# The first attention group's score pieces and row maxima, moved into the QKV projection, and its operands transposed tile by tile

## The reference, cut to what matters

```python
x = L0_attn_hidden_states                      # (2, 1024, 512) f32
x = x + 0.5 * ffn(layernorm(x), w1, mean_w1, w2, mean_w2, w3, mean_w3)
x = x + attn(layernorm(x), w_qkv, b_qkv, w_dense, b_dense)
x = x + 0.5 * ffn(layernorm(x), ...same weights...)

# attn: 32 query heads, 8 key/value heads, head size 16
qkv = einsum('bsh,oh->bso', h, w_qkv) + b_qkv
q, k, v = split(qkv);  q, k = rope(q), rope(k)
scores = einsum('bqhd,bkhd->bhqk', q, k) / 16  # causal mask
probs  = softmax(scores)
out    = einsum('bhqk,bkhd->bqhd', probs, v) @ w_dense.T + b_dense
```

## Time and profile before

| | us |
|---|---|
| median of 3 runs | 1462.23 (1461.75 to 1462.47) |
| the profiled execution, its own time | 1461.78 |
| its span in the trace | 1460.1 |
| PE busy | 1375.6 (94%) |
| DVE busy | 1068.4 (73%) |
| ACT busy | 608.2 (42%) |
| POOL busy | 183.7 (13%) |

### The profile page before, as it was taken

How to read it: one execution, slowest core, us unless ns; L and a number is a source line. 1 busy time by engine, 2 the same in 40 slices (tenths; PEclk the granted TensorE clock), 3 DMA queues, 4 the chain that set the end, 5 groups by cost and what they waited for, 6 DMA issues and landing times.

```text
span 1460.1 us, 25505 instructions
## 1 busy us (share of the span) xinstructions
PE 1375.6 (94%) x9984; PEld 707.6 (48%) x9984; DVE 1068.4 (73%) x1611; ACT 608.2 (42%) x802; POOL 183.7 (13%) x269
## 2 busy tenths in 40 slices
PE   1899999999999996799999999999999999999997
PEld 0344444444444442233333333333577777777774
DVE  7999566764665587899999999965576666665544
ACT  5762123222211352287878777765222122222111
POOL 1000000000000363032323222211011011011000
PEclk9999999999999997599999999999999999999999
DMA  9702941021021012211111111030534647467440
GB/s 386 251 0 101 254 140 58 26 61 44 33 47 36 8 34 42 57 24 30 26 38 24 29 27 38 2 131 1 181 130 156 221 167 217 170 215 204 162 159 29
DMA packets 151980, 144.40 MB, mean 99 GB/s; under 512 B 129856, under 2 KB 133440, under 8 KB 148032
## 3 DMA queue, kind: packets, MB, share of 16 engines
q1 hardware_dynamic: 151872, 142.91, 31.2%
HBM read 96.73 MB, written 21.76 MB: 81 GB/s over the span
## 4 chain that ended last, share of the span: by engine, by line
PE 81%; DVE 11%; ACT 2%; issue 2%; SPq 2%; DMA 1%; POOL 0%; DVEq 0%; ACTq 0%; POOLq 0%
PE ps L2215 17%; PE ps L1778 17%; PE ps L2232 10%; PE ps L1989 9%; PE ps L1903 7%; PE ps L1799 6%; PE ps L1970 5%; PE ps L1893 3%; PE ps L1825 2%; PE ps L2087 2%; DVE rowmax L1534 2%; PE ps L1999 1%; PE ps L1907 1%; DVE blocks L1426 1%; SPq L522 1%
## 5 line engine op out<-in xcount | busy, mean ns | idle before, releaser
L955 ACT ACTIVATE probs<-ps 128x1024 f32<-128x1024 f32 (+3 forms) x384 | 292.5, 811 | 84.0 <-PE ps L1970 82.0
L1778 PE MATMUL ps<-xt_hi,w_all 128*128 128x512 f16 x896 | 274.8, 381 | 9.6 <-DVE w_all L1179 9.3
L2215 PE MATMUL ps<-xs,wpair 128*128 128x256 f16 x2352 | 261.3, 273 | 0.9 <-DVE second_sum L1661 0.9
L2215 PEld LDWEIGHTS ps<-xs,wpair 128*128 128x128 f16 x2352 | 230.1, 98 | 33.5 <-DVE second_sum L1661 1.1
L1534 DVE TENSOR_REDUCE rowmax<-ps 128x2 f32<-128x1024 f32 (+3 forms) x208 | 237.4, 1141 | 11.9 <-PE ps L1911 6.4
L1903 PE MATMUL ps<-ka,qa 48*128 48x512 f16 (+3 forms) x768 | 162.6, 347 | 25.8 <-DVE rowmax L1534 13.1
L1778 PE MATMUL ps<-xt_lo,w_all 128*128 128x512 f16 x448 | 170.5, 381 | 0.0
L1989 PE MATMUL ps<-probs,vs 128*32 128x512 f32 (+3 forms) x1536 | 164.9, 501 | 2.4 <-ACT ctx_sb L974 2.4
L1778 PEld LDWEIGHTS ps<-xt_hi,w_all 128*128 (+1 forms) x896 | 88.0, 98 | 117.4 <-issue 11.4
L1538 DVE TENSOR_REDUCE rowmax<-ps 128x1 f32<-128x512 f32 x192 | 131.1, 683 | 8.1 <-PE ps L1903 8.1
L2232 PE MATMUL ps<-wpair,hs_hi 128*128 128x512 f16 x448 | 133.2, 379 | 0.5 <-DVE hs_lo L1688 0.5
(11 more groups left out here) (168 smaller groups left out, 1811.3 us busy)
## 6 DMA issues: line engine op xcount, KB each, us to landing
wpair<-spill SPq DMA_DIRECT2D x28, 2304.0 KB, 8.9
spill<-block_parts SPq DMA_DIRECT2D x14, 512.0 KB, 2.7
spill<-w_all SPq DMA_DIRECT2D x24, 224.0 KB, 4.1
x<-x_in SPq DMA_DIRECT2D x4, 1024.0 KB, 5.3
y_out<-x SPq DMA_DIRECT2D x4, 1024.0 KB, 11.2
wbase<-m1t SPq DMA_DIRECT2D x4, 896.0 KB, 12.6
w_raw<-w1t SPq DMA_DIRECT2D x4, 896.0 KB, 14.2
wbase<-m3t SPq DMA_DIRECT2D x4, 896.0 KB, 24.2
```

Of the source, the lines that this page charges most:

```text
L955: nc.scalar.activation(probs[u % PBUF][:, 2 * pair:2 * pair + 2, 0:q1 - q0], wide(("scores", g, (u, pair)))[:, :, 0:q1 - q0], ACT.Exp, sca ...
L1778: last = mm(ps[:, bank, :], w[a][:, k, bass.ts(t, P)], xt[b][:, k, :], start=(k == 0 and n == 0), stop=(k == HB - 1 and n == 2))
L2215: last = mm(product_bank(n, i)[:, m, :], weight_of(n, m, a, weight, k), xs[c % 2][:, b, 2 * rows_ + k, :], start=(k == 0 and q == 0), stop ...
```

## The change

QKV tiles 10 to 15 on PE now contain pieces 0 to 16 of group 0: one before the second half of the tile, one after half of that half's matmuls, one behind the tile. DVE reduces pieces 0 to 20 in its loop over the tiles, three in each of the iterations 10 to 16. SP issues group 0's transposes tile by tile as the parts come, between the four pairs of transposes of chunk 7. Pieces 17 to 24 are made, and 21 to 24 reduced, where they were before. The code of each operation is the same; there are as many of each as before.

```diff
+EARLY_TILE = 10
+EARLY_TAKEN = 3 * (TOKEN_TILES + 1 - EARLY_TILE)
+EARLY_MADE = EARLY_TAKEN - 4
...
         sp.wait_ge(up_full, 4 * IT)
-        place_normal(7)
...
-        sp.wait_ge(qklo_ready, 2 * SEQ_TILES)
-        sp.wait_ge(qkhi_ready, 2 * SEQ_TILES)
-        sp.wait_ge(kpad_ready, 4 + SEQ_TILES)
+        def place_first(tt):
+
+            sp.wait_ge(qklo_ready, 2 * tt + 2)
+            sp.wait_ge(qkhi_ready, 2 * tt + 2)
+            sp.wait_ge(kpad_ready, tt + 1 + min(tt // 2 + 1, 4))
+            place_operand_tile(0, tt)
+
+        place_normal_tile(7, 0)
+        sp.wait_ge(qkv_full, 4)
+        place_first(0)
+        place_first(1)
+        place_normal_tile(7, 1)
+        place_first(2)
+        place_first(3)
+        place_normal_tile(7, 2)
+        place_first(4)
+        place_normal_tile(7, 3)
+        for tt in range(5, SEQ_TILES):
+            place_first(tt)
         ln_placed_by(sp, 7)
-        place_operands(0)
         place_operands(1)
...
+        def early(i, at_):
+
+            if i >= EARLY_TILE:
+                reduce_piece(0, 3 * (i - EARLY_TILE) + at_)
+
+        for i in range(TOKEN_TILES + 1):
+            if 3 <= i < 7:
+                normal_parts(7, i - 3)
+            if 1 <= i:
+                add_turned(i - 1)
+            early(i, 0)
+            if i < TOKEN_TILES:
+                along(i)
+            early(i, 1)
+            if 1 <= i:
+                low_parts(i - 1)
+            early(i, 2)
+            if i == 2:
+                norm_stats(7)
...
             for s in range(2):
+                if s:
+                    early_piece(3 * (i - EARLY_TILE) - 1)
...
+                    if s and k == 1:
+                        early_piece(3 * (i - EARLY_TILE))
             last.then_inc(qkv_full, 1)
-
-        for i in range(TOKEN_TILES):
-            qkv(i)
+            early_piece(3 * (i - EARLY_TILE) + 1)
...
+        def early_piece(r):
+
+            if 0 <= r < EARLY_MADE:
+                score_piece(0, r)
+
+        def later_piece(k, r):
+
+            if k or r >= EARLY_MADE:
+                score_piece(k, r)
```

More of the change, by code:

```diff
@@ L488, in _, with place_normal_tile @@
             .then_inc(wd_loaded, 16)
+        def place_normal_tile(n, j):
+            sp.wait_ge(xhi_ready, TPC * n + j + 1)
+            sp.wait_ge(xlo_ready, TPC * n + j + 1)
+            for i in range(2):
+                sp.dma_start_transpose(xt_of(n)[i][:, :, j * P:(j + 1) * P], ln_parts(j)[i])\
+                    .then_inc(ln_placed[n % 2], 16)
         def place_normal(n):
             for j in range(TPC):
[L493 to L497, removed]
+                place_normal_tile(n, j)
         sp.wait_ge(up_full, IT)
@@ L515, in _, with place_operand_tile @@
         sp.wait_ge(up_full, 4 * IT)
-        place_normal(7)
+        def place_operand_tile(g, tt):
+            b, i = divmod(g, KV_HEADS)
+            sp.dma_start_transpose(qa[g % BUF][:, :, tt * P:(tt + 1) * P],
+                                   parts_q[:, SEQ_TILES * b + tt, Q_PER_KV * i:Q_PER_KV * (i + 1), :].rearrange("p h c -> p (h c)"))\
+                .then_inc(qk_placed[g % BUF], 16)
+            if g % 2 == 0:
+                sp.dma_start_transpose(ka[g // 2 % BUF][:, tt * P:(tt + 1) * P].unsqueeze(1),
+                                       parts_k[:, SEQ_TILES * b + tt, i:i + 2, :].rearrange("p h c -> p (h c)"))\
+                    .then_inc(qk_placed[g % BUF], 16)
         def place_operands(g):
-            b, i = divmod(g, KV_HEADS)
             for tt in range(SEQ_TILES):
[L522 to L528, removed]
-        sp.wait_ge(qklo_ready, 2 * SEQ_TILES)
-        sp.wait_ge(qkhi_ready, 2 * SEQ_TILES)
-        sp.wait_ge(kpad_ready, 4 + SEQ_TILES)
+                place_operand_tile(g, tt)
+        def place_first(tt):
[15 more added lines that the diff above has]
+            place_first(tt)
         ln_placed_by(sp, 7)
-        place_operands(0)
         place_operands(1)
@@ L1501, in low_parts @@
                                     in1=parts_k[:, i, :, 0:HEAD], op=ALU.subtract).then_inc(qklo_ready, 1)
[L1503 to L1513, removed]
         def reduce_piece(k, r):
@@ new lines, in _ @@
+        for i in range(TOKEN_TILES + 1):
[13 more added lines that the diff above has]
+        def later_piece(k, r):
+            if k or r >= EARLY_TAKEN:
+                reduce_piece(k, r)
@@ new lines, in _ @@
+        for k in range(GROUPS):
+            later_piece(k, 0)
+            later_piece(k, 1)
+            later_piece(k, 2)
+            later_piece(k, 3)
+            later_piece(k, 4)
+            later_piece(k, 5)
+            later_piece(k, 6)
+            later_piece(k, 7)
+            later_piece(k, 8)
+            later_piece(k, 9)
+            later_piece(k, 10)
+            later_piece(k, 11)
+            later_piece(k, 12)
+            normalise(k - 2, 0)
+            later_piece(k, 13)
+            later_piece(k, 14)
+            later_piece(k, 15)
+            later_piece(k, 16)
+            later_piece(k, 17)
+            later_piece(k, 18)
+            later_piece(k, 19)
+            later_piece(k, 20)
+            later_piece(k, 21)
+            later_piece(k, 22)
+            later_piece(k, 23)
@@ L1604, in _ @@
             normalise(k - 2, 1)
-            reduce_piece(k, 24)
+            later_piece(k, 24)
             split_rowmax(k)
@@ L1945, in score_piece, with later_piece @@
             last.then_inc(single_full, 1)
+        def early_piece(r):
+            if 0 <= r < EARLY_MADE:
+                score_piece(0, r)
+        def later_piece(k, r):
+            if k or r >= EARLY_MADE:
+                score_piece(k, r)
+        for i in range(TOKEN_TILES):
+            qkv(i)
         def transpose_rowmax(g):
@@ L2003, in _ @@
             scores_t(k - 2, 6, 1)
-            score_piece(k, 0)
-            score_piece(k, 1)
+            later_piece(k, 0)
+            later_piece(k, 1)
             scores_t(k - 2, 7, 0)
             values(k - 2, 5)
-            score_piece(k, 2)
+            later_piece(k, 2)
             transpose_rowmax(k - 1)
             scores_t(k - 2, 7, 1)
-            score_piece(k, 3)
+            later_piece(k, 3)
             scores_t(k - 2, 8, 0)
             values(k - 2, 6)
-            score_piece(k, 4)
+            later_piece(k, 4)
             scores_t(k - 2, 8, 1)
             scores_t(k - 2, 9, 0)
-            score_piece(k, 5)
+            later_piece(k, 5)
             values(k - 2, 7)
             scores_t(k - 2, 9, 1)
-            score_piece(k, 6)
+            later_piece(k, 6)
             values(k - 2, 8)
-            score_piece(k, 7)
+            later_piece(k, 7)
             scores_t(k - 2, 10, 0)
-            score_piece(k, 8)
+            later_piece(k, 8)
             scores_t(k - 2, 10, 1)
@@ L2027, in _ @@
             scores_t(k - 2, 11, 0)
-            score_piece(k, 9)
-            score_piece(k, 10)
+            later_piece(k, 9)
+            later_piece(k, 10)
             scores_t(k - 2, 11, 1)
-            score_piece(k, 11)
+            later_piece(k, 11)
             values(k - 2, 10)
-            score_piece(k, 12)
+            later_piece(k, 12)
             scores_t(k - 1, 0, 0)
@@ L2036, in _ @@
             scores_t(k - 1, 0, 1)
-            score_piece(k, 13)
+            later_piece(k, 13)
             scores_t(k - 1, 1, 0)
-            score_piece(k, 14)
+            later_piece(k, 14)
             values(k - 2, 11)
-            score_piece(k, 15)
+            later_piece(k, 15)
             scores_t(k - 1, 1, 1)
             scores_t(k - 1, 2, 0)
-            score_piece(k, 16)
+            later_piece(k, 16)
             values(k - 1, 0)
-            score_piece(k, 17)
+            later_piece(k, 17)
             scores_t(k - 1, 2, 1)
             scores_t(k - 1, 3, 0)
-            score_piece(k, 18)
+            later_piece(k, 18)
             values(k - 1, 1)
             scores_t(k - 1, 3, 1)
-            score_piece(k, 19)
+            later_piece(k, 19)
             scores_t(k - 1, 4, 0)
-            score_piece(k, 20)
+            later_piece(k, 20)
             values(k - 1, 2)
-            score_piece(k, 21)
+            later_piece(k, 21)
             scores_t(k - 1, 4, 1)
-            score_piece(k, 22)
+            later_piece(k, 22)
             scores_t(k - 1, 5, 0)
             values(k - 1, 3)
-            score_piece(k, 23)
+            later_piece(k, 23)
             scores_t(k - 1, 5, 1)
@@ L2064, in _ @@
             scores_t(k - 1, 6, 0)
-            score_piece(k, 24)
+            later_piece(k, 24)
             values(k - 1, 4)
```

24 lines of the change are left out of this document (removed).

## The result

| | us |
|---|---|
| changed kernel, median of 6 runs | 1455.72 (1455.49 to 1456.23) |
| kernel before, median of 6 runs beside it | 1461.99 |
| ratio, 95% interval | 0.9949 (0.9936 to 0.9962) |
| profiled execution, its span | 1455.49, 1453.8 |

The account below looks back on a forecast made before the run. PE was taken to bound the kernel, except at the ends and in a hole at 560 to 620 us; group 1's first reduction coming 7.7 us earlier gave 1462.23 - 7.7 = 1454.5 us, range 1449 to 1458.5.

Parts of the forecast that it names:

- The place and the kind of the gain: Hole between QKV tiles and group pipeline: whole program moves with group 1's first reduction, 7.7 us earlier than 594.23.
- SP and the wait: Piece 0 in tile 10: SP's 24 transposes at 1.28 us land at 539.8, so PE waits 4.3 us.
- The clock inside tile 10: At PE's wait before piece 0: clock falls for 4 to 5 us, so PE does 2.1 us less.
- The woven tiles: Tiles 10 to 15: PE's and DVE's lists equally long, 1.2 us added for mutual waits, tile 15 ends at 573.2.
- The tail: Group 0 behind tile 15: 13.3 us to group 1's first reduction at 586.5, including 0.8 of waits.
- Group 1 unchanged: Group 1: clock expected to fall in group 0's tail, so group 1 takes 28.4 us as before, gain 0.
- One sign: Clock in the profile after: low from about 578 until some 5 us behind the first transposed scores at 598.6.
- The maxima: Group 0's maxima: placements begin at 592.7, land at 596.9, PE wants them at 598.6; 1.7 us slack, next wait.
- (1): Rival: clock stays full through the hole, group 1 up to 4.0 us less; 1448 to 1451.5 us; chance 0.14.
- (2): Rival: woven tiles wait for each other, 6.3 us each instead of 5.6; 1457.5 to 1459 us; chance 0.11.
- (3): Rival: woven tiles run at the half clock, each 5.6 us more; with all five 1482 us; chance 0.07.
- (4): Rival: gain given back at the maxima if SP reaches group 3's transposes 9 us later; 1462 us; chance 0.06.

Follow-up runs that it names:

- e3_keep_busy: Changed kernel with 22 extra matmuls of 512 columns in front of piece 0, where PE waits for the transposes: 1453.38 us, ratio 0.9940.
- e9_maxima_first: Changed kernel with extra matmuls in PE's waits behind the last tile, and SP's two dense-projection loads moved behind the first maxima placement: 1451.96 us.
- e7_tile11_filled: Changed kernel with weaving begun at tile 11 and extra matmuls behind the last tile and in group 1: 1447.70 us, ratio 0.9891.
- e5_filled_tail: Changed kernel with extra matmuls, results not used, in PE's waits behind the last QKV tile and in group 1: 1454.49 us, ratio 0.9944.
- c_after: Changed kernel itself measured once more, with no edit, on another occasion: 1456.57 us, ratio 0.9961.
- e10: Changed kernel with weaving from tile 11, extra matmuls behind the last tile and in group 1, and maxima placed before SP's two loads: 1447.04 us.

## Why the prediction was right, step by step

**The place and the kind of the gain: right.** The program moved by about what the first reductions of group 1 moved: 6.7 us there, 6.3 at the end.

**SP and the wait: right, 0.5 us too short.** 4.3 us were forecast and 4.81 measured, and piece 0 began at 540.70, 0.8 us later than the forecast 539.9. SP was full, as worked out. Group 0's transposes took 1.28 us each, waits of their own included; the chunk's took more, one of them 1.74 us (at 523.57), so that the 24 from 508.05 to 539.50 come to 1.31 each.

**The clock inside tile 10: right.** It fell, and cost 1.2 to 2.3 us (`e3_keep_busy`). It fell later than forecast, 4.6 us behind the last matmul and not 3.2, and PE worked 3.2 us at the half clock, which is 1.6 us lost and not 2.1.

**The woven tiles: right, in part by luck.** Tile 15 ended at 573.31 against 573.2, but two errors cancel in that: tile 10 ended at 543.3 where 542.4 was forecast, and the 0.9 us added for the rest of the half clock was not needed, since the clock was back before tile 11 began. DVE was busy 25.77 of the 28 us from 545 to 573, over 90% as forecast. PE's rows show two waits in them, 0.55 at piece 9 and 0.79 at piece 13, together near the 1.2 us that I had put down for mutual waiting.

**The tail: mis-sized.** This is the term that took most of the missing microsecond. I gave it 13.3 us from tile 15's end to group 1's first reduction (587.51 in DVE's timeline), and it took 14.20. The cosines started on time, at 574.27. Behind them the waits were 0.16 for ACT and 0.17 and 0.87 for pieces 23 and 24, made at the half clock, and around each the overlap of neighbours is lost, about 0.25 in all: 1.45 in place of 0.8. The low parts of tile 14 took 1.53 in place of 1.3, those of tile 15 0.81 in place of 0.9.

**Group 1 unchanged: right, for the reason given.** 28.41 against 28.27, and `e9_maxima_first` and `e7_tile11_filled` show that the clock is the reason. One sign was misread: the clock was to return some 5 us behind the first transposed scores, and it did so at 608.8, 9.2 us behind them; before it was 8.8 (606.28 to 615.1). The 5 us hold from where PE is fully busy, here 604.

**The maxima: right.** They were issued from 593.02 (forecast 592.7) and PE did not wait. The remark that this wait was next was borne out by `e5_filled_tail`, where it opened.

**The rivals.** (1), the clock staying full, did not happen; its price of up to 4.0 us for group 1 was right (28.41 to 24.63 in `e9_maxima_first`). (2) and (3) did not happen: tiles 11 to 15 took 6.0 us each from the end of tile 10's matmuls at 543.3, between the forecast's 5.6 and rival (2)'s 6.3, with 1.3 us of recorded waits on PE and not 3 to 4, and the clock was at 1.00 from 544 on through them. (4) did not happen in this kernel. The rule of the Trainium skill that (3) leaned on (page "TensorE: Matmul & The Clock Gate", section "A second HAM failure mode: psum-queue depth-cycling") did not show in the woven tiles, with waits of 0.55 and 0.79 us in them.

## What to carry to other kernels

Work moved into a busy stage brings its waits with it, and an in-order engine passes them to everything behind. So choose the first place by when the last operand lands: from tile 10 the weaving gave 6.3 us, from tile 11, with less of it, 11.5. And before marks of two profiles are compared to a microsecond, subtract where each stood ahead of the change. Where an engine pair is slow in a thin stage, look at the granted clock before the buffers; here it was worth 3.8 us in one group. Once such a cost is gone, read which wait had the least slack, since it is the next to open.

## What was not expected of the hardware

The clock's fall and return around a wait varied from one execution to the next, the same kernel's too. Four profiles have the wait for the transposes in tile 10 with nothing filled in; the fall is counted from the end of the last matmul, the return from the start of piece 0, all in us and read from their time tables in steps of 0.5:

| profile | wait | fell after | back after | at the half clock |
|---|---|---|---|---|
| changed kernel | 4.81 | 4.6 | 3.2 | 3.4 |
| `c_after` (the same kernel) | 4.90 | 2.0 | 3.9 | 6.8 |
| `e5_filled_tail` | 4.66 | 5.0 | 3.8 | 3.4 |
| `e9_maxima_first` | 5.55 | 4.8 | 6.1 | 6.8 |

In the kernel before it had fallen 3.2 us behind the last matmul. So PE worked 3.2 to 6.1 us at the half clock in this place, and the loss there, half of that, is 1.6 to 3.1 us by execution and not one number.

With PE busy 8.4 of 10 us by short products, one profile kept the full clock and another did not, for almost the same program (`e7`, `e10`). Of the four profiles with the waits behind the last tile filled by extra matmuls, two kept the full clock (`e7`, `e9`) and two lost it for 3.3 and 3.4 us (`e5`, `e10`), where the versions without had it at 1.2 GHz for tens of microseconds: filling kept out the long half clock in these four, and did not exclude a short one.
